# Attention inside a three-stage kernel: the work that uses one shared PSUM bank is moved from the middle of each unit to its end

## The chip, the cores and the metric

The kernel runs on one core of a Trainium2 chip. The metric is the device time of one execution in microseconds (us), lower is better. The engines are TensorE (PE in the rows, its weight loads PEld), VectorE (DVE), ScalarE (ACT), GpSimd (POOL) and SyncE (SP).

## The reference

Sixteen sequences of 512 tokens with 128 features go through a mixture-of-experts block, an attention block and the same mixture-of-experts block again. The change lies in the attention block alone:

```python
x = x + 0.5 * _L0_ffn_ref(_layernorm(x), ...)
x = x + _L0_attn_ref(_layernorm(x), Wq, bq, Wk, bk, Wv, bv, Wo, bo, head_mask)
x = x + 0.5 * _L0_ffn_ref(_layernorm(x), ...)

def _L0_attn_ref(x, ...):                     # 16 heads of 8 features
    q, k, v = ...                             # x @ W.T + b, split into heads
    attn = einsum('bqhd,bkhd->bhqk', q, k) / sqrt(8)
    attn = softmax(attn) * head_mask
    return einsum('bhqk,bkhd->bqhd', attn, v) @ Wo.T + bo
```

## The kernel before

Every engine has an instruction list of its own, written out in full for the sixteen batches (a batch is one sequence), and the engines meet only through semaphores. So the order in which the code issues is the order in which an engine works.

A batch is 16 units (`UNITS`), numbered u. Unit u belongs to head group g = u // 4 (four heads, a "quad") and to key tile t = u % 4. A unit has two halves with two heads each. In each half TensorE computes two kinds of scores:

- `score_exp` (L927): the transposed scores of this unit, with the row maximum already subtracted through extra rows of the packed operands. ScalarE takes their exponential (L1096).
- `score_max` (L941): the plain scores of the unit eight units later (`AHEAD`), of which VectorE takes the row maximum (L1259).

Both write to the same three PSUM score banks in turn: exp, max, exp, max and so on. A bank is free again when its reader is done. Counting back three places, the exp scores of a half wait for the maximum of two halves ago, and the max scores of a half wait for the exponential of one half ago.

`times_values` (L958) multiplies the exponentials of the unit before with the values and sums over the four key tiles in one bank, `p_o`. After each group of four units ScalarE copies that bank (`copy_o`, L1102), and the next group's first `times_values` waits for the copy.

Everything else shares one last bank, `p_x`. Its users are called pieces; a batch has 14, at most one in a unit (`X_USES` names them in order). `turn_max` (L967, four in a batch) transposes the maxima of a head group, `turn_o` (L975, four) the attention output of a group, `turn_norm` (L982) the normalised output, `project_out` (L988) multiplies with Wo, `project_v` (L915) makes the values of the next batch, `turn_x` (L901) transposes the normalised input two batches ahead, and `project_qk` (L907 to L909, two) makes its q and k. Each piece is drained by a ScalarE copy or a VectorE operation placed at a fixed (unit, half), and the next piece waits for that (`x_bank_drained`). The maxima of a group go on through `copy_max` (L1090, ScalarE) and two DMAs that GpSimd issues (L1203) into the packed q operand; unit 4g waits for those of its group. SyncE issues 24 DMAs per batch that pack q and k of the next batch (L864); it begins them when the scores of the batch before are all done.

TensorE's unit in the code before the change is:

```python
for half in range(2):
    score_exp(b, u, half)
    score_max(ahead, v, half)
    if half == 0:
        pieces(b, u, is_first)
    elif u > 0:
        times_values(b, u - 1)
```

Of the kernel before, what the change touches and what calls it, by code (L numbers as in the profile page):

```python
# [742 lines left out]
def attention(nc, w, src, dst):  # L743
# [9 lines left out]
    with ExitStack() as ctx:  # L753
# [140 lines left out]
        def _(pe):  # L894
# [97 lines left out]
            def batch(b, is_first, is_last):  # L992
                a, c = b.step(-1), b.step(1)
                for u in range(UNITS):
# [6 lines left out]
                    for half in range(2):  # L1001
                        score_exp(b, u, half)
                        if there(ahead):
                            score_max(ahead, v, half)
                        if half == 0:
                            pieces(b, u, is_first)
                        elif u > 0:
                            times_values(b, u - 1)
                        elif not is_first:
                            times_values(a, UNITS - 1)  # L1010

            def pieces(b, u, is_first):
                a, c, e = b.step(-1), b.step(1), b.step(2)
                if u == 1:
                    turn_max(b, 1, uses(b, "m1"))
                if not is_first:
                    if u == 2:
                        turn_o(a, 3, uses(b, "o3"))
                    if u == 3:
                        turn_norm(uses(b, "norm"))  # L1020
                    if u == 4:
                        project_out(uses(b, "out"))
                if u == 5:
                    turn_max(b, 2, uses(b, "m2"))
                if u == 6:
                    turn_o(b, 0, uses(b, "o0"))
                if u == 7 and there(c):
                    project_v(uses(b, "v"))
                if u == 8 and there(e):
                    turn_x(e, uses(b, "x"))  # L1030
                if u == 9:
                    turn_max(b, 3, uses(b, "m3"))
                if u == 10:
                    turn_o(b, 1, uses(b, "o1"))
                if u == 11 and there(e):
                    project_qk(e, w.wq, uses(b, "q"))
                if u == 12 and there(e):
                    project_qk(e, w.wk, uses(b, "k"))
                if u == 13 and there(c):
                    turn_max(c, 0, uses(b, "m0"))  # L1040
                if u == 14:
# [23 lines left out]
        def _(act):  # L1065
# [48 lines left out]
            def pieces(b, u, half, is_first):  # L1114
                a, c, e = b.step(-1), b.step(1), b.step(2)
                now = (u, half)
                if now == (1, 0) and not is_first:
                    copy_o(a, 3, uses(a, "o1") + 1)
                if now == (1, 1):
                    copy_max(b, 1, uses(b, "m1"))  # L1120
                if now == (3, 1) and not is_first:
# [3 lines left out]
                if now == (5, 1):  # L1125
                    copy_max(b, 2, uses(b, "m2"))
                if now == (8, 1) and there(e):
                    x_copy(e, uses(b, "x"))
                if now == (9, 0):
                    copy_o(b, 1, 0 if is_first else uses(b, "o3") + 1)  # L1130
                if now == (9, 1):
                    copy_max(b, 3, uses(b, "m3"))
                if now == (10, 0) and there(e):
# [267 lines left out]
```

## Time and profile before

| | us |
|---|---|
| median of 3 runs | 2092.17 (2088.86 to 2097.89) |
| the profiled execution, device time | 2100.33 |
| its span in the profile | 2098.1 |
| attention, first exp scores of batch 0 to those of batch 15 | 647.44 to 1468.51 |
| TensorE, VectorE, ScalarE, GpSimd busy, share of the span | 89%, 71%, 59%, 42% |

The page of the profile divides the span into 40 slices of about 52 us. The attention block lies in slices 13 to 29. A busy TensorE there is not one at its peak: the record of a matmul spans its passage through the array, and neighbours overlap. The line PEclk gives the clock that TensorE was granted, in tenths of the full 2.4 GHz.

### The profile page before, as it was taken

To read this page: it belongs to the slowest core of one execution; us is meant where nothing else is said; L and a number is where in the kernel's file an instruction comes from. 1 tells how busy PE (TensorE), PEld (TensorE's weight loads), DVE (VectorE), ACT (ScalarE), POOL (GpSimd) and SP (SyncE) were. 2 spreads that over 40 slices of the span, in tenths; PEclk is the share of its full clock that TensorE was granted. 3 is DMA by queue.
4 is the path that set the end of the run, shared out by engine and by line. 5 is a ranking of instruction groups with operands and counts; after the bars stand their busy time and mean duration, and the time that the engine had idled before them with its cause. 6 is when DMAs were issued, how large, how long until landed. Compare 5 with 4: busy or idle time off the path is not lost. (4 is left out here: it accounts for less than half of the span.)

```text
span 2098.1 us, 30450 instructions
## 1 busy us (share of the span) xinstructions
PE 1860.1 (89%) x9600; PEld 1108.9 (53%) x9600; DVE 1496.2 (71%) x2379; ACT 1232.2 (59%) x1914; POOL 887.4 (42%) x875
## 2 busy tenths in 40 slices
PE   3999999999937898999999988888859999999999
PEld 2777777777812333333333333333247777777777
DVE  4767777687517878777787777887447768776775
ACT  3566455555513767666676667776635565556654
POOL 2566555655621222222222222221125565556655
PEclk9999999999955989888888889998879999999999
DMA  2000000000032323222223223222010000000000
GB/s 91 21 11 31 27 24 30 10 30 10 16 59 33 47 47 47 47 42 39 41 44 44 41 41 40 53 44 35 12 36 21 31 11 31 20 30 10 30 14 16
DMA packets 43167, 68.57 MB, mean 33 GB/s; under 512 B 9916, under 2 KB 11444, under 8 KB 43060
## 3 DMA queue, kind: packets, MB, share of 16 engines
q1 hardware_dynamic: 38256, 65.15, 15.7%
q0 software_dynamic: 4096, 1.08, 0.3%
q8 instruction: 58, 0.95, 0.2%
q10 hardware_dynamic: 708, 0.98, 0.1%
q14 instruction: 49, 0.40, 0.1%
HBM read 28.36 MB, written 12.58 MB: 20 GB/s over the span
## 5 line engine op out<-in xcount | busy, mean ns | idle before, releaser
L1259 DVE TENSOR_REDUCE attn_neg_max<-attn_p_score 128x2 f32<-128x1024 f32 x512 | 624.8, 1223 | 211.2 <-PE attn_p_score L941 209.1
L572 POOL TENSOR_TENSOR ffn_hid_low<-ffn_hidden,ffn_hid_high 128x512 fp32r<-128x512 f32 x448 | 580.6, 1298 | 454.9 <-ACT ffn_hid_high L512 454.2
L1096 ACT ACTIVATE attn_exps<-attn_p_score 128x1024 f32<-128x1024 f32 x512 | 519.8, 1025 | 286.6 <-PE attn_p_score L927 284.6
L512 ACT ACTIVATE ffn_hid_high<-ffn_hidden 128x512 fp32r<-128x512 f32 x448 | 281.0, 627 | 255.7 <-DVE ffn_hidden L705 254.8
L503 ACT ACTIVATE ffn_silu<-ffn_p_gate 128x512 f32<-128x512 f32 x448 | 264.0, 589 | 207.8 <-PE ffn_p_gate L375 207.5
L698 DVE TENSOR_TENSOR ffn_gated<-ffn_silu,ffn_p_up 128x512 f32<-128x512 f32 x352 | 240.6, 684 | 175.1 <-PE ffn_p_up L375 112.2
L941 PE MATMUL attn_p_score<-k_pack,q_pack 24*128 24x512 f32 x1024 | 283.2, 553 | 57.7 <-ACT attn_exps L1096 33.0
L958 PE MATMUL attn_p_o<-attn_exps,values 128*32 128x512 f32 x2048 | 312.0, 684 | 8.4 <-ACT attn_o_raw L1102 3.3
L927 PE MATMUL attn_p_score<-q_pack,k_pack 26*128 26x512 f32 x1024 | 271.2, 539 | 14.9 <-DMA q_pack<-attn_max_rows 14.6
L927 PEld LDWEIGHTS attn_p_score<-q_pack,k_pack 26*128 26x128 f32 x1024 | 101.4, 198 | 314.7 <-issue 207.5
L705 DVE TENSOR_TENSOR ffn_hidden<-ffn_gated,ffn_p_spread 128x512 f32<-128x512 f32 x352 | 241.2, 685 | 14.9 <-PE ffn_p_spread L416 4.1
L373 PE MATMUL ffn_p_y<-ffn_hid_high,down_high 128*128 128x512 f32 x448 | 186.3, 416 | 34.0 <-POOL ffn_hid_low L572 33.3
L373 PE MATMUL ffn_p_gate<-ffn_xt_high,gate_high 128*128 128x512 f32 x448 | 188.5, 421 | 0.0
L1203 POOL DMA_DIRECT2D q_pack<-attn_max_rows x128 | 74.3, 582 | 265.0 <-ACT attn_max_rows L1090 265.0
L373 PE MATMUL ffn_p_up<-ffn_xt_high,up_high 128*128 128x512 f32 x448 | 180.4, 403 | 2.9 <-DVE ffn_gated L698 2.8
L375 PE MATMUL ffn_p_up<-ffn_xt_low,up_high 128*128 128x512 f32 x448 | 177.5, 396 | 0.0
L375 PE MATMUL ffn_p_gate<-ffn_xt_low,gate_high 128*128 128x512 f32 x448 | 177.2, 396 | 0.0
L375 PE MATMUL ffn_p_y<-ffn_hid_low,down_high 128*128 128x512 f32 x448 | 177.1, 395 | 0.0
L374 PE MATMUL ffn_p_gate<-ffn_xt_high,gate_low 128*128 128x512 f32 x448 | 176.7, 394 | 0.0
L374 PE MATMUL ffn_p_up<-ffn_xt_high,up_low 128*128 128x512 f32 x448 | 176.2, 393 | 0.0
L374 PE MATMUL ffn_p_y<-ffn_hid_high,down_low 128*128 128x512 f32 x448 | 175.4, 391 | 0.0
L941 PEld LDWEIGHTS attn_p_score<-k_pack,q_pack 24*128 24x128 f32 x1024 | 103.9, 201 | 114.9 <-ACT attn_exps L1096 90.6
(146 smaller groups left out, 2220.9 us busy)
## 6 DMA issues: line engine op xcount, KB each, us to landing
q_pack<-attn_q_high SPq DMA_DIRECT2D x128, 64.0 KB
k_pack<-attn_k_high SPq DMA_DIRECT2D x128, 64.0 KB
ffn_x_in<-in_x SPq DMA_DIRECT2D x16, 256.0 KB, 2.8
ffn_x_res<-in_x SPq DMA_DIRECT2D x16, 256.0 KB, 2.8
after_ffn<-ffn_x_out SPq DMA_DIRECT2D x16, 256.0 KB, 2.0
attn_x_in<-after_ffn SPq DMA_DIRECT2D x16, 256.0 KB, 4.6
k_pack<-attn_k_low SPq DMA_DIRECT2D x64, 64.0 KB
q_pack<-attn_q_low SPq DMA_DIRECT2D x64, 64.0 KB
```

Source lines behind the costliest of these rows:

```text
L373: nc.tensor.matmul(out, weights[0], high, start=start, stop=False)
L374: nc.tensor.matmul(out, weights[1], high, start=False, stop=False)
L375: return nc.tensor.matmul(out, weights[0], low, start=False, stop=stop)
L503: nc.scalar.activation(silu[f % 2][0:n, :], p_gate[f % 2][0:n, :], ACT.Silu).then_inc(silu_ready, 1)
L512: nc.scalar.activation(hid_high[s][0:n, :], hidden[s][0:n, :], ACT.Copy).then_inc(high_ready, 1)
L572: nc.gpsimd.tensor_tensor(hid_low[s][0:n, :], hidden[s][0:n, :], hid_high[s][0:n, :].bitcast(F32), ALU.subtract).then_inc(low_ready, 1)
L705: V.tensor_tensor(hidden[slot(b, f)][:], gated[f % 2][:], p_spread[:], ALU.mult).then_inc(weighted_ready, 1)
L927: last = nc.tensor.matmul(score_bank("exp", b, n)[:, i, :], pack["k"][b.par][rows, g, t * P:(t + 1) * P], pack["q"][b.par][rows, g, :], st ...
L941: last = nc.tensor.matmul(score_bank("max", b, n)[:, j % 2, :], pack["q"][b.par][rows, g, t * P:(t + 1) * P], pack["k"][b.par][rows, g, :] ...
L958: last = nc.tensor.matmul(p_o[h * COLS:(h + 1) * COLS, :], values[b.par][:, t, g * QUAD + h, :], exps[(2 * u + h // 2) % len(exps)][:, h % ...
L1096: nc.scalar.activation(exps[n % len(exps)][:], score_bank("exp", b, n)[:], ACT.Exp, scale=inv_sqrt)\
L1259: V.tensor_reduce(neg_max[g % 2][:, j:j + 2, t], score_bank("max", b, n)[:], AX.X, ALU.max, negate=True).then_inc(max_read, 1)
```

## The change

TensorE issues both halves' scores one after the other, then `times_values`, and then the piece. The list of pieces moves one unit down, so that each piece stands at the end of the unit before the one in whose middle it stood: half a unit sooner. The ScalarE copies and VectorE drains move to the first half of the unit in which the piece used to stand, mostly half a unit sooner too. SyncE's list is the same, and so is GpSimd's. Nothing is computed differently.

```diff
@@ tensor, batch
                         score_exp(b, u, half)
                         if there(ahead):
                             score_max(ahead, v, half)
-                        if half == 0:
-                            pieces(b, u, is_first)
-                        elif u > 0:
-                            times_values(b, u - 1)
-                        elif not is_first:
-                            times_values(a, UNITS - 1)
+                    if u > 0:
+                        times_values(b, u - 1)
+                    elif not is_first:
+                        times_values(a, UNITS - 1)
+                    pieces(b, u, is_first)
@@ tensor, pieces
-                if u == 1:
+                if u == 0:
                     turn_max(b, 1, uses(b, "m1"))
                 if not is_first:
+                    if u == 1:
+                        turn_o(a, 3, uses(b, "o3"))
                     if u == 2:
-                        turn_o(a, 3, uses(b, "o3"))
+                        turn_norm(uses(b, "norm"))
                     if u == 3:
-                        turn_norm(uses(b, "norm"))
-                    if u == 4:
                         project_out(uses(b, "out"))
...
@@ scalar, pieces
-                if now == (1, 0) and not is_first:
-                    copy_o(a, 3, uses(a, "o1") + 1)
-                if now == (1, 1):
+                if now == (1, 0):
+                    if not is_first:
+                        copy_o(a, 3, uses(a, "o1") + 1)
                     copy_max(b, 1, uses(b, "m1"))
-                if now == (3, 1) and not is_first:
+                if now == (3, 0) and not is_first:
                     copy_ot(uses(b, "norm"))
...
+                if now == (8, 0) and there(e):
+                    x_copy(e, uses(b, "x"))
                 if now == (8, 1) and there(e):
-                    x_copy(e, uses(b, "x"))
+                    x_high(e, uses(b, "x"))
...
@@ vector, pieces
-                    if now == (2, 1):
+                    if now == (2, 0):
                         normalise(a, NQ - 1, uses(b, "o3"))
-                    if now == (4, 1):
+                    if now == (4, 0):
                         residual(a, uses(b, "out"))
-                if now == (6, 1):
+                if now == (6, 0):
                     normalise(b, 0, uses(b, "o0"))
```

The other pieces follow the same pattern: m2 from unit 5 to 4, o0 from 6 to 5, v from 7 to 6, x from 8 to 7, m3 from 9 to 8, o1 from 10 to 9, q from 11 to 10, k from 12 to 11, m0 from 13 to 12, o2 from 14 to 13.

TensorE around the piece o1 of a batch in the middle, in the program before (exp scores L927, max scores L941, the piece L975, value products L958; this is unit 10 and the head of unit 11):

```order
L927 MATMUL attn_p_score<-q_pack,k_pack 128x512 x2
L941 MATMUL attn_p_score<-k_pack,q_pack 128x512 x2
L975 MATMUL attn_p_x<-ident,attn_o_raw 128x128 x4
L927 MATMUL attn_p_score<-q_pack,k_pack 128x512 x2
L941 MATMUL attn_p_score<-k_pack,q_pack 128x512 x2
L958 MATMUL attn_p_o<-attn_exps,values 32x512 x4
L927 MATMUL attn_p_score<-q_pack,k_pack 128x512 x2
L941 MATMUL attn_p_score<-k_pack,q_pack 128x512 x2
```

The same piece in the changed program, with unit 9 ahead of it and the head of unit 10 behind:

```order
L927 MATMUL attn_p_score<-q_pack,k_pack 128x512 x2
L941 MATMUL attn_p_score<-k_pack,q_pack 128x512 x2
L927 MATMUL attn_p_score<-q_pack,k_pack 128x512 x2
L941 MATMUL attn_p_score<-k_pack,q_pack 128x512 x2
L958 MATMUL attn_p_o<-attn_exps,values 32x512 x4
L975 MATMUL attn_p_x<-ident,attn_o_raw 128x128 x4
L927 MATMUL attn_p_score<-q_pack,k_pack 128x512 x2
L941 MATMUL attn_p_score<-k_pack,q_pack 128x512 x2
```

The four transposes left the place between the two halves' scores and stand between the value products and the next unit's first scores.

ScalarE from the copies of unit 8 to those of unit 9 in the program before (L1069 and L1073 copy the transposed input, L1102 the value products, L1090 the maxima):

```order
L1069 ACTIVATE attn_xt<-attn_p_x 128x512
L1096 ACTIVATE attn_exps<-attn_p_score 128x1024
L1102 ACTIVATE attn_o_raw<-attn_p_o 128x512
L1096 ACTIVATE attn_exps<-attn_p_score 128x1024
L1090 ACTIVATE attn_max_rows<-attn_p_x 32x128
L1096 ACTIVATE attn_exps<-attn_p_score 128x1024
L1073 ACTIVATE attn_xt_high<-attn_xt 128x512
```

And in the changed program, whose line numbers on ScalarE are smaller by one:

```order
L1068 ACTIVATE attn_xt<-attn_p_x 128x512
L1095 ACTIVATE attn_exps<-attn_p_score 128x1024
L1072 ACTIVATE attn_xt_high<-attn_xt 128x512
L1095 ACTIVATE attn_exps<-attn_p_score 128x1024
L1101 ACTIVATE attn_o_raw<-attn_p_o 128x512
L1089 ACTIVATE attn_max_rows<-attn_p_x 32x128
L1095 ACTIVATE attn_exps<-attn_p_score 128x1024
```

The copy of the maxima now stands directly behind the copy of the value products, ahead of the second exponential of unit 9, and the second copy of the input came from unit 10 to the end of unit 8.

## Rows read from the trace of the kernel before

**Rows 1.** The page: the granted clock in 40 slices of the span
```profile
PEclk9999999999955989888888889998879999999999
```

**Rows 2.** Windows: batches 1 to 14; batch 13; a stretch at the low clock
```profile
704.08:1468.51 764.43, 684.14 (x4266) 257.21 (x4262) 598.74 (x729) 523.26 (x650) 196.38 (x316) 0.90 0.29 44
1361.09:1412.86 51.77, 44.63 (x311) 17.23 (x308) 42.95 (x54) 37.72 (x47) 14.52 (x23) 1.00 0.26 43
977.50:998.00 20.50, 20.39 (x91) 7.47 (x91) 12.53 (x23) 9.86 (x12) 4.61 (x7) 0.50 0.56 65
```
The columns are the window, its length, the busy time of PE, PEld, DVE, ACT and POOL, the granted clock, the DMA share and GB/s.

**Rows 3.** Timeline: a unit without a piece, full clock; start us, us
```profile
704.08 0.50 PE L927 MATMUL attn_p_score<-q_pack,k_pack 26*128 26x512 f32 x2
704.08 0.50 PE L941 MATMUL attn_p_score<-k_pack,q_pack 24*128 24x512 f32 x2
704.47 0.50 PE L927 MATMUL attn_p_score<-q_pack,k_pack 26*128 26x512 f32 x2
704.62 1.94 ACT L1096 ACTIVATE attn_exps<-attn_p_score 128x1024 f32<-128x1024 f32 x2 [1.11 <-PE attn_p_score L927]
705.69 0.50 PE L941 MATMUL attn_p_score<-k_pack,q_pack 24*128 24x512 f32 x2 [0.72 <-ACT attn_exps L1096]
706.12 1.06 PE L958 MATMUL attn_p_o<-attn_exps,values 128*32 128x512 f32 x8
707.12 0.50 PE L927 MATMUL attn_p_score<-q_pack,k_pack 26*128 26x512 f32 x2
```

**Rows 4.** Timeline: unit 10 of a batch, a piece in its middle, full clock
```profile
1014.38 0.50 PE L927 MATMUL attn_p_score<-q_pack,k_pack 26*128 26x512 f32 x2
...
1014.81 0.66 PE L975 MATMUL attn_p_x<-ident,attn_o_raw 128*128 128x128 f32 x4
...
1015.40 0.49 PE L927 MATMUL attn_p_score<-q_pack,k_pack 26*128 26x512 f32 x2
...
1017.42 0.50 PE L927 MATMUL attn_p_score<-q_pack,k_pack 26*128 26x512 f32 x2
```

**Rows 5.** Timeline: a small piece and two large ones, and what follows each
```profile
707.56 0.29 PE L967 MATMUL attn_p_x<-ident,attn_max_parts 128*32 128x128 f32 x1
...
707.77 0.49 PE L927 MATMUL attn_p_score<-q_pack,k_pack 26*128 26x512 f32 x2
...
719.60 1.16 PE L988 MATMUL attn_p_x<-wo,attn_ot 128*128 128x128 f32 x8
...
720.69 0.50 PE L927 MATMUL attn_p_score<-q_pack,k_pack 26*128 26x512 f32 x2
...
964.29 0.47 PE L907 MATMUL attn_p_x<-attn_xt_high,wk_high 128*128 128x512 f32 x1 [0.17 <-ACT attn_q_full L1079]
...
965.16 0.50 PE L927 MATMUL attn_p_score<-q_pack,k_pack 26*128 26x512 f32 x2
```

**Rows 6.** Timeline at the low clock: a unit without a piece, one with
```profile
654.28 0.79 PE L927 MATMUL attn_p_score<-q_pack,k_pack 26*128 26x512 f32 x2
...
656.19 0.79 PE L941 MATMUL attn_p_score<-k_pack,q_pack 24*128 24x512 f32 x2 [0.69 <-ACT attn_exps L1096]
...
658.78 0.79 PE L927 MATMUL attn_p_score<-q_pack,k_pack 26*128 26x512 f32 x2
...
984.63 0.79 PE L927 MATMUL attn_p_score<-q_pack,k_pack 26*128 26x512 f32 x2
...
985.36 1.11 PE L975 MATMUL attn_p_x<-ident,attn_o_raw 128*128 128x128 f32 x4
...
989.13 0.79 PE L927 MATMUL attn_p_score<-q_pack,k_pack 26*128 26x512 f32 x2
```

**Rows 7.** Timeline: unit 4's wait for its packed maxima, the longest, and batch 13's
```profile
1216.17 0.59 PE L927 MATMUL attn_p_score<-q_pack,k_pack 26*128 26x512 f32 x2 [3.22 <-DMA q_pack<-attn_max_rows]
...
1377.76 0.50 PE L927 MATMUL attn_p_score<-q_pack,k_pack 26*128 26x512 f32 x2 [1.49 <-DMA q_pack<-attn_max_rows]
```

**Rows 8.** A group of batches 1 to 14: busy, mean ns, idle before, releasers
```profile
L927 PE MATMUL attn_p_score<-q_pack,k_pack 26*128 26x512 f32 x894 | 237.5, 535 | 11.4 <-DMA q_pack<-attn_max_rows 11.2
```

More of the change, by code:

```diff
@@ L1019, in pieces @@
                     if u == 3:
-                        turn_norm(uses(b, "norm"))
-                    if u == 4:
                         project_out(uses(b, "out"))
+                if u == 4:
+                    turn_max(b, 2, uses(b, "m2"))
                 if u == 5:
-                    turn_max(b, 2, uses(b, "m2"))
-                if u == 6:
                     turn_o(b, 0, uses(b, "o0"))
-                if u == 7 and there(c):
+                if u == 6 and there(c):
                     project_v(uses(b, "v"))
-                if u == 8 and there(e):
+                if u == 7 and there(e):
@@ L1030, in pieces @@
                     turn_x(e, uses(b, "x"))
+                if u == 8:
+                    turn_max(b, 3, uses(b, "m3"))
                 if u == 9:
-                    turn_max(b, 3, uses(b, "m3"))
-                if u == 10:
                     turn_o(b, 1, uses(b, "o1"))
+                if u == 10 and there(e):
+                    project_qk(e, w.wq, uses(b, "q"))
                 if u == 11 and there(e):
-                    project_qk(e, w.wq, uses(b, "q"))
-                if u == 12 and there(e):
@@ L1038, in pieces @@
                     project_qk(e, w.wk, uses(b, "k"))
-                if u == 13 and there(c):
+                if u == 12 and there(c):
                     turn_max(c, 0, uses(b, "m0"))
-                if u == 14:
+                if u == 13:
                     turn_o(b, 2, uses(b, "o2"))
@@ L1298, in pieces @@
                 if there(e):
-                    if now == (2, 0):
+                    if now == (1, 0):
                         norm_stats(e)
-                    if now == (3, 0):
+                    if now == (2, 1):
                         norm_var(e)
                 if not is_first:
-                    if now == (2, 1):
+                    if now == (2, 0):
                         normalise(a, NQ - 1, uses(b, "o3"))
-                    if now == (4, 1):
+                    if now == (4, 0):
                         residual(a, uses(b, "out"))
-                if now == (6, 1):
+                if now == (6, 0):
                     normalise(b, 0, uses(b, "o0"))
-                if now == (7, 1) and there(c):
+                if now == (7, 0) and there(c):
                     copy_values(c, uses(b, "v"))
-                if now == (10, 1):
+                if now == (10, 0):
                     normalise(b, 1, uses(b, "o1"))
-                if now == (14, 1):
+                if now == (14, 0):
                     normalise(b, 2, uses(b, "o2"))
```

18 lines of the change are left out of this document (7 added, 11 removed).

## Prediction

> **What bounds the kernel now.** I read the page first. The attention block is the middle stretch, and it is the only part in which the granted clock is uneven: 8s and 9s where the blocks around it have 9s throughout [rows 1]. The change touches nothing outside it. Then I read windows. Batches 1 to 14 take 764.43 us, 54.60 each, at a mean granted clock of 0.90 [rows 2]. Batch 13 ran at the full clock throughout and took 51.77 [rows 2]; in it VectorE is busy for 42.95, ScalarE for 37.72, TensorE for 44.63. No engine is full, so a chain through several engines must set the unit, and the timeline has to say which.
>
> A unit without a piece, at the full clock [rows 3]: exp and max scores start together at 704.08. The exp scores of the second half follow at 704.47. Their max scores wait until 705.69, because their bank is the one that the first exponential reads (two exponentials of 1.94 together began at 704.62). TensorE waits here for 0.72. Then come the value products at 706.12, and the next unit at 707.12. The unit's chain is: to the first exponential 0.54, to the max scores that wait for it 1.07, to the value products 0.43, to the next unit 1.00, together 3.04 us.
>
> A unit with a piece in its middle [rows 4]: scores at 1014.38, four transposes at 1014.81, the second half's exp scores at 1015.40, the next unit at 1017.42. Again 3.04. The transposes hold TensorE for 0.59 and cost nothing, since they stand inside the wait for the exponential. Only the part of a piece that exceeds this room, about 0.76 (705.69 less 704.08 less two score blocks of 0.43), can lengthen a unit.
>
> **The change part by part.** It removes and adds no instruction: 14 pieces per batch are moved. Moved behind the value products, a piece stands on the chain: max scores, value products, piece, next exp scores. The room of 0.76 in the middle stays, now empty in every unit, because it is set by the exponential and not by what TensorE does meanwhile. So each piece costs its full slot.
>
> The slots, from the start of a piece to the start of what follows: transposed maxima 707.56 to 707.77, 0.21; four transposes 1014.81 to 1015.40, 0.59 [rows 4]; a projection in full fp32 719.60 to 720.69, 1.09; one in three passes 964.29 to 965.16, 0.87 [rows 5]. Per batch: 4 x 0.21 + 6 x 0.59 (o four times, norm, x) + 2 x 1.09 (out, v) + 2 x 0.87 (q, k) = 0.84 + 3.54 + 2.18 + 1.74 = 8.30 us.
>
> Against this stand what pieces cost before. Batch 13 less the 1.49 that its unit 4 waited for the packed maxima [rows 7] is 50.3, and 16 x 3.04 is 48.6. The 1.7 between are pieces longer than the room or late in getting their bank, and value products that wait for ScalarE's copy of `p_o`. The first kind disappears, since at a unit's end the drains are long done; the second stays, with the copy at the same place. Between 0 and 1.7 goes away; I take 1.0. A batch at full clock without DMA waits is then 50.3 + 8.3 - 1.0 = 57.6.
>
> The ScalarE and VectorE drains half a unit sooner: ScalarE is busy for 37.72 in batch 13 [rows 2]; less 32 exponentials at 1.94 for two [rows 3] this leaves 6.7 for 15 copies, 0.45 each. A unit with two exponentials and two copies is then 2.9, under the new 3.6 of a unit with transposes. VectorE is busy for 42.95 per batch [rows 2], 2.7 per unit. Both hide under TensorE's longer unit; without that cover a unit would grow by one copy, 0.45. I cost them at nothing. GpSimd's and SyncE's lists are the same, and what they wait for comes sooner or with more time behind it.
>
> The packed maxima of group 1: unit 4 waits for them up to 3.22 [rows 7], 11.2 in the fourteen batches [rows 8], 0.8 each. Units 0 to 3 now carry four pieces (0.21, 0.59, 0.59, 1.09: 2.5 us), and SyncE's packing, behind which these DMAs land, starts at the same place. Most of the wait goes: I take 0.3, with 0 and 0.8 as ends.
>
> **The low clock.** In batches 1 to 14 the mean clock of 0.90 means that about 20% of the time, 153 us or 11 per batch, lay at 1.2 GHz, the rest at 2.4 [rows 2]. A unit at the low level took 4.50 without a piece and 4.50 with the four transposes (654.28 to 658.78, 984.63 to 989.13) [rows 6]. So a low stretch costs 1 - 3.04/4.50 = 32% of its time, 3.6 per batch, which closes the sum: 50.3 + 3.6 + 0.8 = 54.7 against 54.60.
>
> After the change a unit at the low level is 4.5 plus a slot of about 1.7 times that at full clock (the record of the transposes is 1.11 against 0.66) [rows 4, 6]: in units 0 to 3 4.9, 5.5, 5.5 and 6.4, 22.3, against 3.3, 3.8, 3.6 and 4.1, 14.8, at the full level. A low stretch costs 34% of its time. With 11 us per batch that is 3.7, and the batch becomes 57.6 + 3.7 + 0.3 = 61.6, 7.0 more than now.
>
> Will it be 11? In the stretch from 977.50 to 998.00 TensorE was busy for 20.39 of 20.50 us before the clock rose [rows 2]. In batch 0, where units have no piece and wait 0.69 for the exponential, the low level lasted over more units [rows 6]. The change puts such a wait into every unit, at the high level too. I take 16 us per batch, half as much again: 1.7 more. The ends are 0 and most of the batch.
>
> The Trainium skill, TensorE: Matmul & The Clock Gate, section "A second HAM failure mode: psum-queue depth-cycling", tells of a kernel whose TensorE idles briefly between groups of matmuls while it goes round PSUM banks, and whose clock swings between the two levels for it. By that rule alone the low stretches would lengthen rather than stay; it speaks against this change and would bring the third case below, where the bare carry-over of the rows would bring 2200.
>
> **The sum.** Fourteen batches x (7.0 + 1.7) = 122. Batch 15 has nine of the pieces (3 x 0.21 + 5 x 0.59 + 1.09 = 4.7, some of it at the low level, so 5) and batch 0 eleven, six of them small, of which the first lie at the low level: 6. Less about 1 where waits vanish there too: 132. The profiled execution becomes 2100 + 132 = 2232; it lay 8.2 over the median of the runs shown, so the forecast is 2092.2 + 132 = 2224 us.
>
> **The rivals.**
> 1. The low stretches vanish. For it: batch 13 shows that the alignment of a batch decides it, and the new batch has another length. Against it: idle room in each unit. Then 14 x (57.9 - 54.6) + 10 = 56, 2148 us. With less low time than now but some, up to 2190.
> 2. Low stretches last much longer, half the batch: 30 us x 0.34 = 10 per batch, 14 x (57.9 + 10 - 54.6) + 12 = 198, 2290; throughout, 16 x 4.5 + 14 for the slots at that level = 86 per batch, 14 x 32 + 30 = 478, 2570.
> 3. Faster. The maxima are turned half a unit sooner, so the wait of unit 4 goes (11), the low stretches that follow it and those around units 15 and 0 go (50), and the pieces find other cover. That ends at 2092 - 61 = 2031. It decides where the pieces' exposure is under 61/14 = 4.4 us per batch, half of the 8.3. Against it: the 0.72 wait for the exponential stays where it is [rows 3], ahead of the piece, and nothing in the rows lets the first exp scores of a unit pass a piece in TensorE's list.
> 4. The move changes nothing, because the chain through ScalarE or VectorE binds instead of TensorE's list. Rows 3 and 4 would have to end otherwise: TensorE starts the next unit 1.00 after its value products began, without any wait. Then 2092.
>
> **How the numbers follow.** Forecast (low time from as now to double it, 2195 to 2255): 52%. More low time (2255 to 2400): 18%, over 2400: 7%. Less or none (2140 to 2195): 17%. Nothing: 3%. Faster: 3%. To leave out no more than two in ten I go from 2148 (no low time) to 2330. A change of under 0.5%, 10 us, is about what a measurement of this kernel can't tell from none. Slower by more than that: 94%.
>
> **What would show it.** In the timeline of a unit at full clock with transposes: scores, scores, a wait of 0.7 for the exponential, value products, transposes, and 3.6 between unit starts, not 3.04. A unit without a piece stays at 3.04, one with a projection takes 3.9 to 4.2. TensorE's wait for exponentials ahead of L941 grows, and the wait for the packed maxima shrinks below 5 us in all. Windows at the full clock give 57 to 58 per batch. The prediction is wrong if units with pieces stay near 3.04, or if the clock stays at one level throughout attention.

## The result, and the profile after

The changed kernel takes 2185.05 us (median of 4 runs, 2177.66 to 2195.3) against 2095.03 for the kernel before in the same session: ratio 1.0436, interval 1.0374 to 1.0498, 90 us slower. Forecast were 2224, within 2148 to 2330. The profiled execution took 2195.3 (forecast 2232). The ratios below leave out executions more than 1.5% above the fastest of their kernel, and the medians don't: two of the four in experiment 2, one each in 1, 5 and 6.

The page of the changed kernel: TensorE's busy share, the granted clock [rows 1], and the group of the max scores (busy us, mean ns | idle before).

```profile
PE 1833.4 (84%) x9569; PEld 1094.1 (50%) x9600; DVE 1497.2 (68%) x2379; ACT 1223.3 (56%) x1914; POOL 887.3 (40%) x875
PEclk9999999999857889889989988998779999999999
L941 PE MATMUL attn_p_score<-k_pack,q_pack 24*128 24x512 f32 x1024 | 277.8, 543 | 220.7 <-ACT attn_exps L1095 204.4
```

The same group on the page of before:

```profile
L941 PE MATMUL attn_p_score<-k_pack,q_pack 24*128 24x512 f32 x1024 | 283.2, 553 | 57.7 <-ACT attn_exps L1096 33.0
```

TensorE is less busy in a longer span: it waits. The idle time ahead of the max scores (L941) went from 57.7 us to 220.7, nearly all of it for exponentials.

The view of [rows 8] for batches 1 to 14 of the changed kernel:

```profile
L941 PE MATMUL attn_p_score<-k_pack,q_pack 24*128 24x512 f32 x896 | 239.3, 531 | 186.0 <-ACT attn_exps L1095 186.0
L927 PE MATMUL attn_p_score<-q_pack,k_pack 26*128 26x512 f32 x896 | 183.5, 480 | 0.0
```

Here the wait for the packed maxima is gone: 0.0 against 11.4.

Windows of the changed kernel, the columns as in [rows 2]: batches 1 to 14, and batch 12.

```profile
713.76:1567.54 853.78, 664.28 (x4278) 244.69 (x4274) 601.37 (x731) 517.25 (x652) 195.83 (x315) 0.91 0.25 40
1383.50:1441.10 57.60, 43.74 (x310) 16.64 (x306) 43.05 (x54) 37.17 (x47) 14.50 (x23) 1.00 0.25 43
```

The window of [rows 2] over batches 1 to 14 of the kernel before ends at 1468.51, at the second half of unit 15 of batch 14. Batch 15 begins 2.64 us later:

```profile
704.08:1471.15 767.07, 686.06 (x4279) 257.74 (x4276) 601.16 (x732) 525.20 (x652) 196.38 (x316) 0.90 0.29 45
```

So a batch now takes 853.78 / 14 = 60.98 us on average against 767.07 / 14 = 54.79, 6.2 more. A batch wholly at the full clock takes 57.60, the forecast to the tenth; VectorE and ScalarE are about as busy in it as in the batch of [rows 2] (43.05 and 37.17 us against 42.95 and 37.72), so nothing was added to them. The mean clock of 0.91 means 18% of the time at 1.2 GHz, 154 us or 11 per batch, about as before.

The timeline of the changed kernel, with a unit that carries transposes and part of one with a projection at the full clock, and a unit with the small piece at the low clock, in the order of their times:

```profile
1138.06 0.79 PE L927 MATMUL attn_p_score<-q_pack,k_pack 26*128 26x512 f32 x2
...
1140.70 1.94 PE L958 MATMUL attn_p_o<-attn_exps,values 128*32 128x512 f32 x8
1142.56 0.40 PE L967 MATMUL attn_p_x<-ident,attn_max_parts 128*32 128x128 f32 x1
1142.89 0.79 PE L927 MATMUL attn_p_score<-q_pack,k_pack 26*128 26x512 f32 x2
...
1417.94 0.50 PE L941 MATMUL attn_p_score<-k_pack,q_pack 24*128 24x512 f32 x2 [0.88 <-ACT attn_exps L1095]
1418.52 1.06 PE L958 MATMUL attn_p_o<-attn_exps,values 128*32 128x512 f32 x8
1419.52 0.66 PE L975 MATMUL attn_p_x<-ident,attn_o_raw 128*128 128x128 f32 x4
1420.11 0.50 PE L927 MATMUL attn_p_score<-q_pack,k_pack 26*128 26x512 f32 x2
...
1421.73 0.50 PE L941 MATMUL attn_p_score<-k_pack,q_pack 24*128 24x512 f32 x2 [0.87 <-ACT attn_exps L1095]
1422.16 1.06 PE L958 MATMUL attn_p_o<-attn_exps,values 128*32 128x512 f32 x8
1423.15 0.50 PE L907 MATMUL attn_p_x<-attn_xt_high,wq_high 128*128 128x512 f32 x1
...
1424.05 0.50 PE L927 MATMUL attn_p_score<-q_pack,k_pack 26*128 26x512 f32 x2
```

Read it against [rows 3, 4]. Value products to next unit's scores was 1.00; now the transposes stand between, 1418.52 to 1420.11, 1.59. The wait of 0.88 for the exponential is there in full ahead of it. The last unit is 1420.11 to 1424.05, 3.94, with 0.90 for the q projection. At the low clock the unit with the small piece takes 1138.06 to 1142.89, 4.83.

### The profile page after: what moved, and what is told of

It is laid out like the page before. It is cut to its first block and busy times, and to the rows that moved or that the text cites. A ratio compares the mean times of both kernels' runs of the same rounds, so it can differ in the third digit from the quotient of the medians.

```text
span 2193.1 us, 30419 instructions
## 1 busy us (share of the span) xinstructions
PE 1833.4 (84%) x9569; PEld 1094.1 (50%) x9600; DVE 1497.2 (68%) x2379; ACT 1223.3 (56%) x1914; POOL 887.3 (40%) x875
## 5 line engine op out<-in xcount | busy, mean ns | idle before, releaser
L1095 ACT ACTIVATE attn_exps<-attn_p_score 128x1024 f32<-128x1024 f32 x512 | 508.0, 1021 | 390.1 <-PE attn_p_score L927 390.1
L941 PE MATMUL attn_p_score<-k_pack,q_pack 24*128 24x512 f32 x1024 | 277.8, 543 | 220.7 <-ACT attn_exps L1095 204.4
L958 PE MATMUL attn_p_o<-attn_exps,values 128*32 128x512 f32 x2048 | 306.6, 673 | 9.1 <-ACT attn_o_raw L1101 3.7
L941 PEld LDWEIGHTS attn_p_score<-k_pack,q_pack 24*128 24x128 f32 x1024 | 102.3, 198 | 337.1 <-ACT attn_exps L1095 314.4
L927 PE MATMUL attn_p_score<-q_pack,k_pack 26*128 26x512 f32 x1024 | 210.2, 487 | 3.6 <-DMA q_pack<-attn_max_rows 3.3
L1191 POOL TENSOR_TENSOR attn_max_parts<-attn_neg_max,zeros 128x16 fp32r<-128x16 f32 x64 | 13.9, 218 | 345.3 <-DVE attn_neg_max L1256 345.3
```

The lines of the kernel that those rows point to most:

```text
L941: last = nc.tensor.matmul(score_bank("max", b, n)[:, j % 2, :], pack["q"][b.par][rows, g, t * P:(t + 1) * P], pack["k"][b.par][rows, g, :] ...
L958: last = nc.tensor.matmul(p_o[h * COLS:(h + 1) * COLS, :], values[b.par][:, t, g * QUAD + h, :], exps[(2 * u + h // 2) % len(exps)][:, h % ...
L1095: nc.scalar.activation(exps[n % len(exps)][:], score_bank("exp", b, n)[:], ACT.Exp, scale=inv_sqrt)\
```

## The experiments

The theory of the prediction is a chain in series: whatever stands behind a unit's value products is paid in full, whatever stands in the wait for the exponential is hidden up to its room. Its rivals are that the drains' new places, or the clock, carry the difference.

**1. The drains alone.** TensorE's list as before, the ScalarE and VectorE lists as in the changed kernel.

```diff
-                    if u > 0:
-                        times_values(b, u - 1)
-                    elif not is_first:
-                        times_values(a, UNITS - 1)
-                    pieces(b, u, is_first)
+                        if half == 0:
+                            pieces(b, u, is_first)
+                        elif u > 0:
+                            times_values(b, u - 1)
...
```

> TensorE's list is that of before (pieces in the middle of a unit); the ScalarE copies and VectorE drains stand where the changed kernel has them. Series theory (a piece costs its slot once it stands outside the wait for the exponential): nothing of the cost is in the drains, so the time is that of before, 2095 us within 10, perhaps 5 to 10 less because the maxima of group 1 are copied sooner. Drains theory (two copies in a row ahead of a unit's second exponential, or a drain ahead of a maximum, hold up the next scores): most of the 90 us, 2150 to 2185.

Measured: 2095.92 us, ratio 1.001 (0.9959 to 1.0062). In the whole the earlier drains gain nothing that can be measured. Two windows of this run, batches 1 to 14 and batch 9 (wholly at the full clock), and the timeline of unit 4 of batch 9, with the output projection:

```profile
703.35:1465.10 761.75, 708.14 (x4278) 263.65 (x4274) 602.76 (x732) 527.51 (x652) 196.83 (x318) 0.87 0.29 45
1138.11:1189.18 51.07, 45.44 (x311) 17.43 (x308) 42.86 (x54) 37.84 (x47) 14.50 (x23) 1.00 0.31 48
```

```profile
1150.85 0.50 PE L927 MATMUL attn_p_score<-q_pack,k_pack 26*128 26x512 f32 x2 [0.38 <-DMA q_pack<-attn_max_rows]
...
1151.28 1.16 PE L988 MATMUL attn_p_x<-wo,attn_ot 128*128 128x128 f32 x8
...
1153.89 0.50 PE L927 MATMUL attn_p_score<-q_pack,k_pack 26*128 26x512 f32 x2
```

The unit takes 3.04: the 1.09 of this projection cost no more than the 0.59 of the transposes, though the prediction saw room for 0.76 only. The units with v, q and k take 3.04, 3.04 and 3.05 at the full clock, where the kernel before took 3.41, 3.28 and 3.16 (medians of the starts of exp scores). So the drains do save something. Batch 9 takes 51.07, of which 1.67 are two waits for packed maxima (0.38 in unit 4, 1.29 in unit 8), and the 49.4 left are 0.9 under the 50.3 of before. The whole doesn't show it, because batches 1 to 14 had a clock of 0.87 instead of 0.90 [rows 2]: 198 us at the low level for 153, and 45 x 0.32 = 14 us is about what fourteen batches save (14 x 0.9 = 13). The step from this run to the changed kernel, 2185.05 less 2095.92, is TensorE's list alone: 89 us, give or take some 10 by the interval.

**2. The piece behind the second half's exp scores** (kernel before otherwise): still between scores, still ahead of the value products.

```diff
                         score_exp(b, u, half)
+                        if half == 1:
+                            pieces(b, u, is_first)
                         if there(ahead):
                             score_max(ahead, v, half)
```

> The kernel before with each piece one step later: behind the second half's exp scores, ahead of its max scores, still inside the wait for the exponential. Drains as before. Series theory: maxima and transposes fit into the 0.76 of room, so units with them stay at 3.04; the four projections push the second max scores, which now no longer run beside the exp scores: up to 0.4 each, 1.6 per batch, 25 us at most: 2090 to 2120. Theory that a piece costs wherever it leaves the middle between the two halves: near the changed kernel, 2185.

Measured: 2169.43 us (2141.3 to 2190.53), ratio 1.025 (1.019 to 1.0309), outside the 2090 to 2120 expected. The chain is not where it went. The timeline of this run, a unit with transposes at the low clock and one at the full clock, and a window over batches 1 to 14:

```profile
840.72 0.79 PE L927 MATMUL attn_p_score<-q_pack,k_pack 26*128 26x512 f32 x2
...
841.88 1.11 PE L975 MATMUL attn_p_x<-ident,attn_o_raw 128*128 128x128 f32 x4
842.92 0.79 PE L941 MATMUL attn_p_score<-k_pack,q_pack 24*128 24x512 f32 x2
...
845.51 0.79 PE L927 MATMUL attn_p_score<-q_pack,k_pack 26*128 26x512 f32 x2
...
1418.47 0.50 PE L927 MATMUL attn_p_score<-q_pack,k_pack 26*128 26x512 f32 x2
...
1419.15 0.66 PE L975 MATMUL attn_p_x<-ident,attn_o_raw 128*128 128x128 f32 x4
1420.10 0.50 PE L941 MATMUL attn_p_score<-k_pack,q_pack 24*128 24x512 f32 x2 [0.28 <-ACT attn_exps L1098]
...
1421.52 0.50 PE L927 MATMUL attn_p_score<-q_pack,k_pack 26*128 26x512 f32 x2
```

```profile
715.50:1559.71 844.21, 764.53 (x4278) 279.75 (x4274) 604.47 (x732) 517.44 (x652) 196.73 (x318) 0.79 0.25 41
```

At the full clock the unit is 3.05, as in [rows 4]: the piece fills part of the wait of this place. At the low clock it is 4.79 against 4.50 in [rows 6]. The clock is 0.79 where before it was 0.90: 42% of the 844 us at the low level, over twice the 153 of before. Some 200 us more at 0.32 to 0.35 are 64 to 70 us, most of the 77 by which this window is longer than the 767.07 of before. (The profiled execution is the slowest of the four, 2190.53; the other times can't be divided like this.) So a piece that is hidden at the full clock is not free where the clock is low for longer. How its place does that isn't shown.

**3. The piece ahead of the value products** (changed kernel otherwise). The same work in series, two neighbours swapped.

```diff
+                    pieces(b, u, is_first)
                     if u > 0:
                         times_values(b, u - 1)
                     elif not is_first:
                         times_values(a, UNITS - 1)
-                    pieces(b, u, is_first)
```

> The changed kernel with the piece ahead of the value products and behind the second max scores. Series theory: the same chain in another order, so 2185 us within 10, units with four transposes at 3.63, without a piece at 3.04. Theory that the place directly behind the value products is what costs (a bank written right behind another, or the first scores of the next unit held up behind a transpose): clearly under 2185, towards 2140 or less.

Measured: 2482.98 us, ratio 1.1811 (1.1769 to 1.1854), 300 us away from what the chain gives. The page, a window and the timeline of this run:

```profile
PEclk9999999996555656565565555665576899999999
```

```profile
730.00:1800.00 1070.00, 903.14 (x4012) 299.85 (x4004) 567.10 (x693) 486.05 (x616) 190.21 (x301) 0.59 0.18 30
```

```profile
748.66 0.50 PE L941 MATMUL attn_p_score<-k_pack,q_pack 24*128 24x512 f32 x2 [0.89 <-ACT attn_exps L1095]
749.60 0.27 PE L967 MATMUL attn_p_x<-ident,attn_max_parts 128*32 128x128 f32 x1 [0.43 <-DVE attn_x_out L1281]
749.80 1.49 PE L958 MATMUL attn_p_o<-attn_exps,values 128*32 128x512 f32 x8
```

A mean clock of 0.59 is 82% of the time at the low level, 877 of 1070 us. The rows of the timeline show a second wait in this unit: the piece now stands closer behind the one before it and waits 0.43 for that one's drain on VectorE, after the 0.89 for the exponential. The value products behind it already run at the low level in part (1.49 for 1.06). But this wait comes only 15 times, 6.5 us in all, and all waits of pieces for a drain add to about 19 us in this run; by their own length they are little in 300.

**4. The room filled, changed kernel.** The second half's exp scores are issued twice into the same bank in each unit, so TensorE works where it waited. The repeat is redundant work; the output is the same.

```diff
+    FILL = lambda u: True
...
-                for i in range(2):
+                for i in (0, 1, 0, 1) if half == 1 and FILL(u) else (0, 1):
```

> The changed kernel, with the exp scores of each unit's second half computed twice into the same bank (redundant work, nothing left out), the repeat of 0.43 us inside the 0.76 wait for the exponential. Series theory with the clock as a separate term: units at the full clock stay as they are, 57.6 per batch; the low stretches, 3.4 us per batch now, go or shrink, so 2135 to 2150 us, granted clock in attention near 1. If the low stretches don't come from the idle room of the units, the time stays at 2185 or rises a little through the repeat at the low level.

Measured: 2143.8 us, ratio 1.0217 (1.0194 to 1.024), 41 less than the changed kernel, by more work. A window of one batch and one of batches 1 to 14, and the timeline (lines are one higher):

```profile
768.15:825.78 57.63, 47.51 (x342) 19.38 (x339) 43.07 (x54) 37.19 (x47) 14.54 (x23) 1.00 0.29 44
710.53:1514.83 804.30, 663.18 (x4728) 269.82 (x4724) 601.40 (x732) 517.42 (x652) 196.52 (x316) 1.00 0.27 43
```

```profile
768.15 0.50 PE L928 MATMUL attn_p_score<-q_pack,k_pack 26*128 26x512 f32 x2
...
768.55 0.73 PE L928 MATMUL attn_p_score<-q_pack,k_pack 26*128 26x512 f32 x4
769.77 0.50 PE L942 MATMUL attn_p_score<-k_pack,q_pack 24*128 24x512 f32 x2 [0.49 <-ACT attn_exps L1096]
```

The wait shrank from 0.88 to 0.49, and all fourteen batches ran at 1.00. Thirteen took 57.6 each; batch 14 took 55.24, as there is no batch 16 for which it would carry x, q and k (slots of 0.59 + 2 x 0.87 = 2.33). This is the undisturbed chain of the changed kernel, and 853.78 - 804.30 = 49 us is what the low stretches cost it in the profile.

**5. The room filled, kernel before,** in units 0, 1, 5, 9, 13 and 15, where a small piece or none leaves it.

```diff
+    FILL = lambda u: u in (0, 1, 5, 9, 13, UNITS - 1)
```

> The kernel before with the same repeat of the second half's exp scores (redundant work) in the units that have room for it: 0, 15 and those with transposed maxima in the middle. With the filled changed kernel (2143.8 us) it makes a pair without the low stretches. Series theory: a batch at the full clock is 50.3 plus 1 to 3 of waiting for the packed maxima in unit 4, so 2045 to 2075 us, and the pair differs by 70 to 100, of which the clock has no part. If the change cost mainly through the clock, the pair would differ by 40 or less.

Measured: 2098.32 us, ratio 0.999 (0.9866 to 1.0114); expected were 2045 to 2075. A window over batches 1 to 14 and the group of the exp scores in it:

```profile
706.73:1468.44 761.71, 677.28 (x4446) 260.96 (x4442) 601.82 (x732) 526.87 (x652) 196.47 (x316) 0.94 0.29 45
```

```profile
L928 PE MATMUL attn_p_score<-q_pack,k_pack 26*128 26x512 f32 x1064 | 252.6, 503 | 25.1 <-DMA q_pack<-attn_max_rows 25.1
```

The clock rose from 0.90 to 0.94: 92 us at the low level instead of 153, worth 61 x 0.32 = 20. But the wait for the packed maxima rose from 11.2 [rows 8] to 25.1, by 14. Units 0 to 3 ran faster and came earlier to unit 4, whose maxima land no sooner. The fourteen batches took 761.71 for 767.07, 5 us less, which is about the 6 that are left; batch 0 (59.53 for 56.63 us) and what lies behind batch 14 (2.4 more) took them back. So in the kernel before a part of the low stretches costs nothing, because it lies in units that would wait at unit 4 instead.

The pair of filled kernels was to differ by 70 to 100 us if the chain is in series and by 40 or less if the clock is what costs. It differs by 45, which decides nothing as it stands, since the filled kernel before still has low stretches and longer waits. With these taken off (92 x 0.32 = 29 and 25.1), the fourteen batches of the pair, 804.30 and 761.71, lie 97 us apart. The chain gives 14 x 7.3 less the 2.3 of batch 14, 100.

**6. The same as 4, order of experiment 3.**

```diff
+    FILL = lambda u: True
...
-                for i in range(2):
+                for i in (0, 1, 0, 1) if half == 1 and FILL(u) else (0, 1):
```

> The kernel with the piece ahead of the value products (2483 us, about two thirds of attention at the low clock) with the repeat in every unit. Clock theory: its extra 300 us over the changed kernel is the low clock alone, brought on because pieces that need a drain of the same unit now wait 0.2 to 0.5 more for it; filled, the clock stays high and the batch is 57.6 plus 1 to 2, so 2155 to 2185. Theory that the place itself costs (the chain through the value products is longer there at any clock): stays over 2300. If the fill does not hold the clock, in between, with the windows showing it.

Measured: 2433.21 us, ratio 1.1592 (1.1447 to 1.1737); expected were 2155 to 2185. The window of 730 to 1800 shows a clock of 0.60 and TensorE busy for 975 instead of 903 us. It is of the slowest of the four executions, 2485.56; the others took 2411.6 to 2442.85, so the repeat took some 50 us off. What removed the low stretches in experiment 4 doesn't in this order.

**7. Only the transposes at the end.** Changed kernel, with the pieces of projections and maxima back in the middle, the room filled where no piece or the small one stands there.

```diff
+    FILL = lambda u: u == 0 or PIECE[u - 1] in AT_END + (None,) or PIECE[u - 1][0] == 'm'
+    PIECE = X_USES + (None, None)
+    AT_END = ('o3', 'norm', 'o0', 'x', 'o1', 'o2')
...
+                        if half == 0 and u > 0 and PIECE[u - 1] not in AT_END:
+                            pieces(b, u - 1, is_first)
...
-                    pieces(b, u, is_first)
+                    if PIECE[u] in AT_END:
+                        pieces(b, u, is_first)
```

> Drains as in the changed kernel; of the pieces only the six with four transposes (o, norm, x) stand at a unit's end, the other eight in the middle as before; the repeat of exp scores fills the units whose middle has room. Series theory, by slots: 6 x 0.59 = 3.5 per batch over the filled kernel before, less 0.3 for norm, so 50.3 + 3.3 plus a wait of under 1 in unit 4: about 54 per batch and 2085 to 2105 us; units with a transpose at the end 3.63, units with a projection in the middle 3.04 to 3.1, because its drain comes sooner. If the cost is not additive by slot, it leaves this range.

Measured: 2098.41 us, ratio 1.0034 (0.994 to 1.0129), within the 2085 to 2105 expected. A window of one batch's length at the full clock:

```profile
812.72:865.48 52.76, 46.94 (x334) 18.82 (x330) 43.04 (x53) 37.40 (x47) 14.51 (x23) 1.00 0.27 47
```

52.76 less the 3.54 of six transposes is 49.2, near the 49.4 that a batch with hidden pieces and the same drains took in experiment 1. The step from there to 57.60 is 4.84, and the slots of four small pieces and four projections are 0.84 + 2.18 + 1.74 = 4.76. The slots add up one by one. In the whole the transposes at the end cost nothing that can be measured, but only together with the repeat and the new drains: the low level is rarer here (a mean clock of 0.954 over the span, 0.929 in the kernel before), which pays for a part of them.

**8. The value products in the middle, the piece at the end.** If a piece is hidden in the wait, the long block may be hidden there and the piece come behind it. The ScalarE copies of `p_o` come one unit sooner.

```diff
                         if there(ahead):
                             score_max(ahead, v, half)
-                    if u > 0:
-                        times_values(b, u - 1)
...
+                        if half == 0:
+                            if u > 0:
+                                times_values(b, u - 1)
...
                     pieces(b, u, is_first)
```

> The changed kernel with the value products of the unit before in the middle (scores, value products, scores, piece), and the copies of p_o one unit sooner, in the unit in which the group's last value products now are. The 1.00 us of value products is put under the wait for the exponential in place of a piece. Series theory: the exponential's 1.6 from the first scores covers scores 0.43 and value products 1.00, then scores 0.43 and the piece, 2.05 plus slot; the maxima on VectorE, 43 us per batch, then bind at 2.7 per unit. The wait for the packed maxima in unit 4 grows to about 4.5 since SyncE's packing still takes 15.5 from a batch's start. About 48 per batch at the full clock, and with low stretches at most 52: 1975 to 2060 us, faster than both. Theory that only the whole amount of TensorE work counts (it is 84 to 89% busy): no faster than before, 2095.

Measured: 2130.06 us, ratio 1.0151 (1.004 to 1.0262), far from 1975 to 2060. The profiled execution took 2104.2 at a clock of 0.929 over the span, the other three 2129.58 to 2133.42 at 0.912 or 0.913; why they differ isn't known. The timeline:

```profile
946.42 1.06 PE L958 MATMUL attn_p_o<-attn_exps,values 128*32 128x512 f32 x8
947.41 0.50 PE L927 MATMUL attn_p_score<-q_pack,k_pack 26*128 26x512 f32 x2
...
947.85 0.66 PE L975 MATMUL attn_p_x<-ident,attn_o_raw 128*128 128x128 f32 x4
948.43 0.50 PE L927 MATMUL attn_p_score<-q_pack,k_pack 26*128 26x512 f32 x2
949.03 0.50 PE L941 MATMUL attn_p_score<-k_pack,q_pack 24*128 24x512 f32 x2
949.46 1.06 PE L958 MATMUL attn_p_o<-attn_exps,values 128*32 128x512 f32 x8
950.46 0.50 PE L927 MATMUL attn_p_score<-q_pack,k_pack 26*128 26x512 f32 x2
```

From 947.41 to 950.46 is 3.05: this is the unit of before, shifted by half a unit. The miss corrects the picture of the chain. Max scores of either half wait for the exponential of one half ago, so TensorE's list has two waits per unit, one ahead of each half's max scores. In the kernel before and in this one the value block stands behind one and the piece behind the other, and a unit takes 2.04 + 1.00 as long as the piece is not much longer than the value block (0.59 here, up to 1.09 in experiment 1). A clearly longer piece should set the pace itself; no run has one. In the changed kernel both stand behind the same wait: 2.04 + 1.00 + piece, 3.63 for transposes. So what matters is not middle or end, but whether the piece and the value block stand on opposite sides of a score pair. This order has no gain over the kernel before: its batch 5, at the full clock throughout, takes 50.58 (929.47 to 980.05), where before it is 50.3.

**9 to 11. SyncE's packing later.** Experiment 5 left the question whether the 24 packing DMAs, behind which the packed maxima land, set a floor of about 54 us per batch under the kernel before. SyncE waits until the maxima of group 1 have landed (9); with the rooms filled as in 5 (10); with the drains of experiment 1 as well (11).

```diff
                 if there(b, 1):
+                    sp.wait_ge(max_packed[1], b.count(MAX_DMA * NQ // 2, MAX_DMA))
                     pack_block(c, "q", 0)
```

> The kernel before; SyncE begins a batch's 24 packing DMAs only when the packed maxima of group 1 have landed. Theory of the common floor (units 0 to 3 of the kernel before can't take less than about 15.5 us, because unit 4 waits for maxima that land behind the packing; so its low stretches there cost little): with the floor gone the batch falls to 50.3 where the clock stays high, but the low stretches of 3.6 per batch stay and now cost in full; 2070 to 2095 us, the waits of unit 4 under 5 in all. Theory that those DMA waits are an independent cost of 0.8 per batch: 2083 and nothing more to be had with the repeat.

> The kernel before with both: the repeat of exp scores in the units that have room (redundant work), which alone gave 2098, and the packing begun later. Theory of the common floor: both together free what neither does alone, 50.3 to 51.3 per batch, 2035 to 2060 us. Theory of independent costs: the sum of the single effects, 2080 or more.

> As the one before, with the ScalarE copies and VectorE drains of the changed kernel while TensorE's pieces stay in the middle. With the drains alone, units with a projection took 3.04 in place of 3.16 to 3.41 at the full clock, 1 us per batch: 2020 to 2050 us, 10 to 15 under the run before it. If a drain in the first half holds up an exponential or a maximum that matters, no gain.

Measured: 2260.01 (ratio 1.0777, 1.0727 to 1.0827), 2253.98 (1.0762, 1.0715 to 1.0809) and 2238.08 (1.0713, 1.0642 to 1.0783), 165 to 220 above what was expected. The waits of TensorE in the first of them (us in all, times, longest; "issue" is a wait for which the view names no releaser):

```profile
PE attn_p_score L928 <- issue: 93.8, 10, 12.2
...
PE attn_p_score L928 <- DMA q_pack<-attn_max_rows: 27.6, 5, 6.0
```

The new wait, 9.4 us a time and up to 12.2 (and the five for packed maxima), stands at the head of unit 8, where TensorE waits in its list for the packed operands of the next batch. SyncE's first packing DMA, in a batch that it entered at 967.72, was issued at 978.62, 11 us later, and the last four from 992.93 on; unit 8 could go on only at 1006.51. But the old wait is gone: no unit 4 of batches 1 to 14 waits for its maxima in any of the three. In run 10 units 0 to 3, all at the full clock, took 12.46 or 12.47 us in thirteen of these batches (12.28 in the last). One of them:

```profile
711.19:723.66 12.47, 10.92 (x81) 3.88 (x77) 10.83 (x22) 8.46 (x10) 1.68 (x5) 1.00 0.04 15
```

In experiment 5, with the packing at its old place, they took 12.96 to 15.28 up to unit 4's first scores, the wait for its maxima in it. So the packing is what the maxima of group 1 land behind, and without it the first units are not held to the 15.5 that the expectation of experiment 9 names (the kernel before has batches with 13.36 and 14.03 too). Whether a whole batch would then come down to 50.3 these runs can't say, because unit 8 waits instead.

**12. Experiment 3, with VectorE's drain ahead of the unit's first maximum,** so that the piece no longer waits for it.

```diff
                     for half in range(2):
+                        if half == 0:
+                            pieces(b, (u, half), is_first)
                         if there(ahead):
                             take_max(ahead, v, half)
-                        pieces(b, (u, half), is_first)
+                        if half == 1:
+                            pieces(b, (u, half), is_first)
```

> The kernel with the piece ahead of the value products (2483 us), with VectorE's drain ahead of the unit's first maximum in place of behind it. If the waits of a piece for its drain (0.2 to 0.5 in the units with norm, m2, v, x and q), added to the wait for the exponential, keep the clock low there: the low time in attention falls from about 960 us to under 400 and the time to 2180 to 2300. If the clock stays low all the same, the place of the piece between the idle room and the value products is what keeps it low, not the drains: 2400 or more.

Measured: 2365.38 us, ratio 1.1254 (1.1183 to 1.1326), between the two expectations. A window of this run:

```profile
730.00:1700.00 970.00, 788.59 (x4105) 278.18 (x4105) 585.74 (x702) 496.54 (x627) 191.92 (x306) 0.72 0.20 34
```

The clock went from 0.59 to 0.72: 56% of the time at the low level instead of 82%. Moving one engine's drains took back 118 of the 298 us by which experiment 3 lay over the changed kernel, and through the clock: the waits for VectorE that went add to about 11 us, and a wait of the transposes for ScalarE's copy of the maxima grew from 2.5 to 9.4. 180 remain, and the clock of 0.72 against 0.91 goes with them; what keeps it low is not explained.

## Why the prediction was right, and what was off

**The chain** was right. Forecast was a full-clock batch of 57.6, from 50.3 + 8.3 - 1.0; measured 57.60 and, with the rooms filled, 57.6 in thirteen of fourteen. Its parts add up: transposes alone give 52.76 (experiment 7). The signs named came: 3.63 for a unit with transposes (3.74 to 3.78 where ScalarE's copy of `p_o` falls into it too), 3.04 without a piece, 3.94 with q or k, 4.13 with out or v (starts of exp scores in the timeline). The wait ahead of L941 grew to 186.0 us in batches 1 to 14.

**Two readings were off, without harm to the sum.** The 1.0 per batch that goes away was put down to the pieces' new place, and the drains were costed at nothing. Experiment 1 leaves the pieces in the middle, and the drains alone bring 0.9. And the room of 0.76 in the middle was too small: 1.09 is hidden there. The forecast doesn't hang on it, since it moves the pieces out of that room altogether.

**The mis-sized term** is the low-clock time. The carry-over of 11 us per batch was raised to 16 because of the idle room in every unit; it stayed at 11. That is 1.7 x 14 = 24 us of the 37 by which the forecast for the profiled execution was high (2232 against 2195.3). Five smaller ones make up the rest. Low stretches cost (853.78 - 804.30) / 14 = 3.5 per batch where the carry-over alone gave 3.7, 2 us. The wait for the packed maxima was left at 0.3 per batch and is 0.0, 4 us. Batch 14 has no x, q and k and was charged for them, 2 us. The batch of before was taken as 54.60, from a window that ended half a unit early, and is 54.79, 3 us. The ends became 8 us longer for the 10 that were taken, 2 us, and not as forecast: batch 0 went from 56.63 to 65.83 (9.2 for 6; only four of its eleven pieces are small, not six, and their slots make 6.0 at the full clock already), while batch 15 with all behind it became 1.4 shorter instead of 5 longer.

**The rule on depth-cycling** (the Trainium skill, TensorE: Matmul & The Clock Gate, section "A second HAM failure mode: psum-queue depth-cycling") would have lengthened the low stretches. (The prediction calls that the third case; it means its second rival.) By the rows it didn't come about in this order: 0.91 against 0.90, with a wait of 0.88 in each unit. Experiment 4 goes its way (0.49 of wait, a clock of 1.00), experiments 3 and 6 show that the wait in a unit alone doesn't decide.

**The rivals.** The vanished low stretches came true only with the rooms filled: 2143.8 against the 2148 worked out. Low throughout, 86 us per batch, is near what experiment 3 did by another order (79 to 83 in batches 1 to 13). Rival 3 was half right: the wait of unit 4 went, as it said, but the low stretches that it tied to it stayed, and the exposure was 7.3 per batch, not under 4.4.

**What stays open.** What lets the clock fall and rise at a given alignment isn't settled. Seven orders of the same matmuls had mean clocks in batches 1 to 14 of 0.91 (changed), 0.90 (before), 0.89 (experiment 8), 0.87 (1), 0.79 (2), 0.71 (12) and 0.60 (3); the place of VectorE's drains has a part in it (experiment 12). That the changed kernel kept the low time of before is therefore luck in part: the prediction's reason, a carry-over, is not one that would have told it from experiment 3. Also open is whether something holds the kernel before at some 54 us per batch when its low stretches are taken away: experiment 5 gives 50.3 + 25.1/14 + 0.32 x 92/14 = 54.2 (measured 761.71 / 14 = 54.4), so a wait and the low stretches account for it, but no run took both away without a new wait.

## What to carry to other kernels

In an in-order list that waits twice per unit for the same slow reader, put side work behind one wait and the long block behind the other: side work no longer than the block is then hidden, here 3.04 instead of 3.63 for a unit. Count a piece's whole slot, start to start of what follows, and check the sum on a batch that ran at one clock level. Before taking a hidden wait or a low stretch away, see what the units behind it would wait for next, since in experiments 5 and 9 to 11 the next wait took the gain or more.

## What the runs showed of the hardware

- The order of neighbouring work alone moved the mean granted clock in attention from 0.91 to 0.59 and the time from 2185 to 2483 us, with the same number of matmuls. This was not expected.
- More work made the kernel faster: repeating one pair of score matmuls per unit took 41 us off (2185.05 to 2143.8), since the clock stayed at 1.00 for 804 us. In another order the same repeat left it at 0.60 in the profiled execution.
- The low level costs a block of value products 1.94 for 1.06 us, but a unit without a piece only 4.50 for 3.04, a ratio of 1.48, since ScalarE's two exponentials take 1.94 at either level (655.12 in the kernel before, and [rows 3]). A unit with the small piece at its end took 4.83 for 3.26, the same ratio.
